# Layer 2's closing moved into its relu attention, with two chunks of the shared expert in the attention's end

## The chip, the cores and the metric

One NeuronCore of a Trainium2 chip runs the whole kernel as one launch. Its engines are TensorE (PE in the profile; its weight loads are PEld), VectorE (DVE), ScalarE (ACT), GpSimd (POOL) and the sync engine (SP), which here issues most DMA transfers. The metric is the device time of one execution in microseconds (us); lower is better. TensorE's clock has two levels, 1.2 and 2.4 GHz; the profile gives the granted clock as a share of the upper one, so that 0.50 is the lower level.

## The reference

A language-model tower of two layers on 4096 tokens (4 sequences of 1024) of width D = 192, all in float32. The change touches layer 2 alone:

```python
h = h + _L1_attn_ref(_layernorm(h), ...)   # relu ("performer") attention, 12 heads, 64 features:
    qp = relu(q @ projection.T) + 0.001;  kp = relu(k @ projection.T) + 0.001
    context = sum over tokens of kp x v;  out = (qp @ context) / (qp @ sum of kp)
    return out @ w_proj.T + b_proj                 # the output projection
h = h + _L1_ffn_ref(_layernorm(h), ...)    # mixture of experts:
    scores = softmax(xf @ w_router.T)              # router logits, top 2 of 8 experts
    out = routed + swiglu(xf; sg, su, sd)          # the shared expert: every token goes through it
```

## The kernel before

Tokens stand 128 to a tile, four tiles (CT) to a chunk of 512 (CHUNK), eight chunks (CHUNKS). The residual stream `h` stays in SBUF. Stages follow one another with a barrier of all engines between them. Each stage first takes its semaphores; SP sets each to its start value before the barrier. Inside a stage each engine has its own instruction list, written out in the source in a fixed order, and waits on semaphores; every engine works strictly in that order.

Layer 2 has four stages.

- `relu_attention`: a loop over chunks c, written out. In turn c TensorE makes the key features of c (`k_features`), turns a finished context (`turn_context`, only in even turns), projects queries and keys of c+1 (`project_qk`), forms the outputs of chunk c-2 (`outputs`), the query features of c in two halves of four and two pairs of heads (`q_features`), the values of c+1 (`project_v`), transposes the normed input of c+2, and adds chunk c to the context (`accumulate`). VectorE takes the key features out of PSUM with the relu, reads the context, norms chunk c+2 (`prepare`), divides chunk c-2 (`divide`, twice two tiles) and takes the query features out. ScalarE copies the projections and takes the square roots of the norm. Six PSUM banks form a ring: every unit of work (`qk`, `kf`, `qf`, `out`, `v`, `ct`) takes the next bank in one written order and waits until the unit that held it has been read. Banks 6 and 7 serve the transposes and the context.
- `close_attention`: projects the attention's rows with `w1_out`, adds them to `h`, norms the sum into `x2`, writes it to DRAM for the routed experts' gather, turns it (`transpose_x2`, into the shared expert's input `sh.xt`) and computes the router's logits. It works through eight chunks; layer 1 has the same stage. SP also loads the expert weights here.
- `route`: softmax, top 2, and the tables of which token goes into which block, almost all on VectorE. Beside it TensorE, ScalarE and GpSimd run chunks 0 and 1 of the shared expert. VectorE builds the rows of a table into `TABLE_BUFS` = 16 buffers, and TensorE multiplies them in between the shared units.
- `experts`: first shared chunk 2 (`ahead`), then a loop over pairs of blocks for the routed experts, then the tail: shared chunks 3 to 7 (`behind`), and for all eight chunks the mixing (`mix`) of the routed rows into `h`, which SP loads from DRAM into two buffers (`BUFS`), and the stores of the result.

A shared chunk is three units (24 in all). A unit is `shared_up` (four matmuls over 512 tokens), a silu on ScalarE, a product, and `shared_down`. In the tail VectorE's order is set by this rule, and SP loads chunk c+2's rows only after mixing chunk c:

```python
for n in behind:
    shared_product(nc, dve, s, n)
    if f == 0 and chunk > SHARED_AHEAD:
        shared_add(nc, dve, s, chunk - 1)
        until = min(CHUNKS, 2 * (chunk - SHARED_AHEAD))
        for c in range(chunks_mixed, until): mix(c)
for c in range(chunks_mixed, CHUNKS): mix(c)
```

Of the kernel before, what the change touches and what calls it, by code (L numbers as in the profile page):

```python
# [24 lines left out]
P = 128  # L25
# [25 lines left out]
SHARED_IN_ROUTE = 2  # L51
SHARED_AHEAD = 3
# [61 lines left out]
def pipeline(eng, turns, start, step, finish, unrolled=False):  # L114
# [8 lines left out]
    if unrolled:  # L123
        for i in range(turns - 1):
            turn(i)
    else:
        with eng.Fori(0, turns - 1) as i:
            turn(i)
    step((1, turns - 1), (0, turns - 1), None)
    finish()  # L130
# [552 lines left out]
def close_attention(nc, a, s, layer):  # L683

    with ExitStack() as ctx:
        new_sem = ctx.enter_context(semaphores(nc))

        def sb(name, shape, dt=F32):
            return ctx.enter_context(nc.sbuf_tensor(f"ca{layer}_" + name, shape, dt))

        h, attn, ps = s.h, s.attn, s.psum
        router = a[f"w{layer}_router"]
# [9 lines left out]
        if layer == 0:  # L702
            x2_t = sb("x2_t", [P, 2, 2, CHUNK])
        XB = P if layer == 0 else DB
        RB_AT = 0 if layer == 0 else DB
# [5 lines left out]
        weights, ones, chain = (new_sem(f"ca{layer}_{n}") for n in ("weights", "ones", "chain"))  # L711
        two = {n: [new_sem(f"ca{layer}_{n}{u}") for u in range(2)] for n in
# [10 lines left out]
        def x2_cols(u, k, w, rows_of=slice(0, P), j=0, n=CHUNK):  # L723

            if layer == 0:
                return x2_t[rows_of, u, w, j:j + n]
            first = k * S + (u * CHUNK + j)
            return s.shared.xt[rows_of, w, slice(first, first + n) if isinstance(k, int) else bass.ds(first, n)]

        @block.sync  # L730
        def _(sp):
            for dst, src in ((wo_a[:], a[f"w{layer}_out"][0:P, :]), (wo_b[:], a[f"w{layer}_out"][P:D + 1, :]),
                             (wr_a[:], router[0:P, :]), (wr_b[RB_AT:RB_AT + RB], router[P:, :])):
                sp.dma_start(dst, src).then_inc(weights, 16)
# [4 lines left out]
            tokens = s.x_tokens[layer].rearrange("(t p) d -> p t d", p=P)  # L739
# [24 lines left out]
        def _(dve):  # L764
            nc.vector.memset(rows_tb[DB:DB + 1, :, :], 1.0).then_inc(ones, 1)
            if layer == 0:
                nc.vector.memset(x2_t[DB:DB + 1, :, 1, :], 1.0).then_inc(ones, 1)

            def copy_x2(u, k):
                dve.wait_ge(two["x2_ps"][u], START + k + 1)  # L770
                dve.wait_ge(two["logits_ps"][u], START + k)
                rows_of = slice(0, DB if layer == 0 else P)
                nc.vector.tensor_copy(x2_cols(u, k, 1, rows_of), ps[rows_of, PS_XB, :]).then_inc(two["x2_dve"][u], 1)
# [36 lines left out]
        def _(act):  # L810
# [6 lines left out]
            def copy_x2(u, k):  # L817
                act.wait_ge(two["x2_ps"][u], START + k + 1)
                act.wait_ge(two["logits_ps"][u], START + k)
                nc.scalar.copy(x2_cols(u, k, 0), ps[:, PS_XA, :]).then_inc(two["x2_act"][u], 1)  # L820
# [10 lines left out]
            def start():  # L831

                act.wait_ge(ones, START + 2 - layer)
                copy_rows(0, 0)
# [3 lines left out]
        def _(pe):  # L838
            pe.wait_ge(weights, START + 64)
            pe.wait_ge(ones, START + 2 - layer)  # L840

            def transposes(src, bank_a, bank_b, first_b=P):
                for j in range(CT):
                    nc.tensor.transpose(ps[:, bank_a, j * P:(j + 1) * P], src[:, j, 0:P], s.ident[:])
                    last = nc.tensor.transpose(ps[0:D - first_b, bank_b, j * P:(j + 1) * P], src[:, j, first_b:D],
                                               s.ident[:])
# [8 lines left out]
            def transpose_x2(u, k):  # L855
# [3 lines left out]
                transposes(x2[:, u], PS_XA, PS_XB, XB).then_inc(two["x2_ps"][u], 1)  # L859
# [13 lines left out]
            def compute_logits(u, k):  # L873
# [3 lines left out]
                for j in range(CT):  # L877
                    dst = ps[:, PS_L, j * E:(j + 1) * E]
                    rows_of = slice(RB_AT, RB_AT + RB)
                    nc.tensor.matmul(dst, x2_cols(u, k, 0, slice(0, P), j * P, P), wr_a[:], start=True, stop=False)  # L880
                    last = nc.tensor.matmul(dst, x2_cols(u, k, 1, rows_of, j * P, P), wr_b[rows_of],
# [15 lines left out]
            pipeline(pe, B, lambda: transpose_rows(0, 0), step, finish, unrolled=(layer == 1))  # L897


class SharedExpert:  # L900
# [3 lines left out]
    PS_GATE, PS_UP, PS_Y = 1, 3, 5  # L904

    def __init__(self, sb, new_sem):
        self.xt = sb("xt", [P, 2, T])
        self.silu = sb("silu", [P, 2, CHUNK])
        self.up = sb("up", [P, 2, CHUNK])
        self.g = sb("g", [P, 2, CHUNK])  # L910
        self.y = sb("y", [P, CT * D])
        (self.gate_ps, self.up_ps, self.silu_done, self.up_left, self.g_done, self.down_done, self.y_copied,
         self.y_added) = (new_sem("sh_" + n) for n in (
             "gate_ps", "up_ps", "silu", "up_left", "g", "down", "y_copied", "y_added"))

    def units(self, first, last):

        return range(first * self.PARTS, last * self.PARTS)


def shared_up(nc, pe, s, n):
# [3 lines left out]
    gate, up = ps[:, sh.PS_GATE + n % 2, :], ps[:, sh.PS_UP + n % 2, :]  # L925
# [3 lines left out]
    pe.wait_ge(sh.g_done, START + n - 1 if n else START)  # L929
    nc.tensor.matmul(gate, s.up_a[:, 0, E, cols], x[0], start=True, stop=False)  # L930
    nc.tensor.matmul(up, s.up_a[:, 1, E, cols], x[1], start=True, stop=False)  # L931
    nc.tensor.matmul(gate, s.up_b[HIGH, E, cols], x[1][HIGH], start=False, stop=True).then_inc(sh.gate_ps, 1)  # L932
    nc.tensor.matmul(up, s.up_b[LOW, E, cols], x[0][LOW], start=False, stop=True).then_inc(sh.up_ps, 1)


def shared_down(nc, pe, s, n):

    sh, ps = s.shared, s.psum
    chunk, f = divmod(n, sh.PARTS)
    if f == 0:  # L940
# [1239 lines left out]
```

## Time and profile before

| | us |
|---|---|
| median of three runs | 1840.75 |
| the three runs | 1835.26 to 1847.22 |
| the profiled execution, its own time | 1849.49 |
| its span, first to last instruction | 1847.8 |
| busy in the span: TensorE / VectorE / ScalarE / GpSimd | 1621.7 / 1098.9 / 613.7 / 429.0 |

The busy times are shares of the whole span; the stages have different limits, so what a change in one stage is worth is read from that stage. Idle time of an engine that nothing waits for costs nothing.

### The profile page before, as it was taken

Reading aid. Unit: us, or ns where it says so; the run is one execution under the profiler, and the core shown is the slowest. Engines: PE = TensorE matmul, PEld = TensorE weight load, DVE = VectorE, ACT = ScalarE, POOL = GpSimd, SP = SyncE. Lnnn points to the kernel's source line nnn. Section 1 sums busy time; section 2 is a strip of 40 time slices with the busy share of each in tenths; the row PEclk is TensorE's granted clock in tenths of the full one; section 3 lists DMA queues with packets and bytes.
Section 4 is the critical chain, followed back from the end, with each engine's and each line's share of the span. In section 5 each row is a group of like instructions: output and inputs, shape, how many; then the busy total and the mean of one; then the engine's idle time right before and its main releaser. Section 6 shows DMA issues by size and latency. Waiting matters only on the chain. (4 is left out here: it accounts for less than half of the span.)

```text
span 1847.8 us, 28783 instructions
## 1 busy us (share of the span) xinstructions
PE 1621.7 (88%) x8964; PEld 889.3 (48%) x8965; DVE 1098.9 (59%) x2504; ACT 613.7 (33%) x826; POOL 429.0 (23%) x526
## 2 busy tenths in 40 slices
PE   5759999999899999675999918899699799999998
PEld 3411332233233232473666604667696656666654
DVE  5868998899799891365333335565355823333345
ACT  3411666566566668211111102111012112222111
POOL 6540000000000000101555414000001246666620
PEclk9765999899999999875999958999766799999999
DMA  2480222022222200720111121000420011111124
GB/s 81 148 142 12 35 35 33 4 35 34 35 34 35 35 1 1 212 64 7 39 40 41 36 60 43 2 1 2 120 100 26 1 30 53 52 51 52 46 81 147
DMA packets 64239, 92.82 MB, mean 50 GB/s; under 512 B 9809, under 2 KB 49556, under 8 KB 63124
## 3 DMA queue, kind: packets, MB, share of 16 engines
q1 hardware_dynamic: 50912, 65.08, 15.6%
q0 software_dynamic: 12288, 25.18, 4.6%
q10 hardware_dynamic: 960, 1.57, 0.5%
q8 instruction: 41, 0.67, 0.2%
q14 instruction: 38, 0.31, 0.1%
HBM read 61.82 MB, written 29.98 MB: 50 GB/s over the span
## 5 line engine op out<-in xcount | busy, mean ns | idle before, releaser
L510 DVE TENSOR_REDUCE sa_half_max<-psum 128x1 f32<-128x512 f32 x768 | 494.7, 688 | 79.9 <-PE psum L613 60.0
L567 ACT ACTIVATE sa_probs<-psum 128x1024 f32<-128x1024 f32 x384 | 372.5, 1021 | 168.1 <-PE psum L604 166.6
L613 PE MATMUL psum<-k_stack,q_stack 96*128 96x512 bf16 x768 | 286.4, 411 | 28.8 <-PEq L404 18.8
L604 PE MATMUL psum<-q_stack,k_stack 97*128 97x512 bf16 x768 | 232.1, 386 | 6.1 <-ACT sa_probs L567 5.4
L613 PEld LDWEIGHTS psum<-k_stack,q_stack 96*128 96x128 bf16 x768 | 75.2, 98 | 285.0 <-issue 153.1
L636 PE MATMUL psum<-sa_probs,sa_v_ext 128*32 128x512 f32 x1536 | 207.4, 612 | 0.6 <-ACT sa_probs L567 0.6
L1541 PE MATMUL psum<-w_e_up_a,ex_xt 128*128 x448 | 171.4, 525 | 0.0
L1405 ACT ACTIVATE ex_silu<-psum 128x384 f32<-128x384 f32 (+1 forms) x112 | 59.3, 529 | 289.4 <-PE psum L1541 286.9
L1557 PE MATMUL psum<-w_e_down,ex_g_t 128*128 x752 | 137.2, 334 | 0.5 <-DVE ex_g_t L1437 0.5
L1557 PEld LDWEIGHTS psum<-w_e_down,ex_g_t 128*128 128x128 f32 x752 | 120.7, 190 | 34.5 <-issue 34.5
L1445 DVE COPY ex_to_rows<-slot_rows 128x2 uint32 (+1 forms) x56 | 10.3, 184 | 211.6 <-DMA y_rows<-ex_y,ex_to_rows 117.5
L1347 POOL DMA_INDIRECT y_rows<-ex_y,ex_to_rows x112 | 110.3, 985 | 97.2 <-DVE ex_y L1446 69.1
L1316 POOL DMA_INDIRECT ex_x<-x_tokens,ex_tokens x112 | 110.7, 988 | 55.7 <-POOL ex_tokens L1322 40.1
L1430 DVE TENSOR_TENSOR ex_g<-ex_silu,psum 128x384 f32<-128x384 f32 (+1 forms) x112 | 67.1, 602 | 94.9 <-PE psum L1541 85.1
L499 POOL COPY sa_v_ext<-v_nat 128x512 f32 x12 | 7.2, 612 | 479.1 <-PE psum L636 478.7
L604 PEld LDWEIGHTS psum<-q_stack,k_stack 97*128 97x128 bf16 x768 | 72.8, 99 | 88.7 <-ACT sa_probs L567 28.9
L1541 PEld LDWEIGHTS psum<-w_e_up_a,ex_xt 128*128 128x128 f32 x448 | 83.7, 191 | 59.6 <-issue 31.0
L755 POOL COPY ca_rows<-attn 128x768 f32 (+1 forms) x16 | 13.2, 827 | 407.1 <-POOLq L715 311.8
L1534 PE MATMUL psum<-ex_w_b,ex_xt 64*128 64x384 f32 (+1 forms) x448 | 98.2, 557 | 3.1 <-ACT ex_xt L1399 2.3
L1399 ACT COPY ex_xt<-psum 128x512 f32<-128x512 f32 x56 | 32.8, 586 | 127.2 <-PE psum L1523 127.2
L1437 DVE COPY ex_g_t<-psum 128x384 f32<-128x384 f32 (+1 forms) x112 | 63.9, 605 | 17.3 <-PE psum L1548 14.7
L636 PEld LDWEIGHTS psum<-sa_probs,sa_v_ext 128*32 128x32 f32 x1536 | 30.4, 108 | 81.6 <-issue 75.5
(267 smaller groups left out, 2257.0 us busy)
## 6 DMA issues: line engine op xcount, KB each, us to landing
q_stack<-qk_parts SPq DMA_DIRECT2D x66, 128.0 KB, 4.5
k_stack<-qk_parts SPq DMA_DIRECT2D x66, 128.0 KB, 7.2
qk_parts<-ep_parts SPq DMA_DIRECT2D x16, 384.0 KB, 3.4
x_tokens<-x SPq DMA_DIRECT2D x16, 384.0 KB, 2.6
ex_rows<-y_rows SPq DMA_DIRECT2D x16, 384.0 KB, 4.7
qk_parts<-ep_parts SPq DMA_DIRECT2D x16, 192.0 KB, 4.3
w_e_down<-e_down SPq DMA_DIRECT2D x1, 3072.0 KB, 32.7
ra_rows<-y_rows SPq DMA_DIRECT2D x8, 384.0 KB, 3.3
```

Of the source, the lines that this page charges most:

```text
L510: nc.vector.tensor_reduce(half_max[:, g, hd, qt, half:half + 1], slot, AX.X, ALU.max).then_inc(ring_free[r], 1)
L567: nc.scalar.activation(probs[:, st % 2, 2 * pair:2 * pair + 2, :], ps[:, 2 * pair:2 * pair + 2, :], ACT.Exp, scale=SCALE0).then_inc(exp_do ...
L604: last = nc.tensor.matmul(ps[:, hd, :], kst[:, g, hd, kt * P:(kt + 1) * P], qst[:, g, hd, half * HALF:(half + 1) * HALF], start=True, stop ...
L613: last = nc.tensor.matmul(ps[:, 4 + r, :], qst[0:SK, g, hd, qt * P:(qt + 1) * P], kst[0:SK, g, hd, half * 512:(half + 1) * 512], start=Tru ...
L636: last = nc.tensor.matmul(ps[hd * W:(hd + 1) * W, OUT, :], v_ext[:, g, kt, hd, :], probs[:, st % 2, hd, :], start=(kt == 0), stop=(kt == T ...
L1316: pool.indirect_dma_start(out=x[:, u, :], out_offset=None, in_=x_tokens, in_offset=bass.IndirectOffsetOnAxis(ap=tokens[:, u:u + 1], axis=0 ...
L1347: pool.indirect_dma_start(out=y_rows, out_offset=bass.IndirectOffsetOnAxis(ap=to_rows[:, u:u + 1], axis=0), in_=y[:, u, :], in_offset=None ...
L1430: nc.vector.tensor_tensor(g[:, u, :], silu[:, u, :], ps[:, PS_UP + u, 0:F], ALU.mult).then_inc(g_done, 1)
L1437: nc.vector.tensor_copy(g_t[:, u, :], ps[:, PS_G + u, 0:F]).then_inc(g_t_done, 1)
L1534: last = nc.tensor.matmul(ps[:, bank + u, 0:F], xt[rows_of, u, v, :], w_b[rows_of, u, :], start=True, stop=False)
L1541: nc.tensor.matmul(ps[:, bank + u, 0:F], xt[:, u, v, :], w.up(u, v), start=False, stop=True).then_inc(done, 1)
L1557: last = nc.tensor.matmul(ps[:, PS_Y, u * D:(u + 1) * D], g_t[:, u, c * P:(c + 1) * P], w.down(u, c), start=(c == 0), stop=(c == FC - 1))
```

## The change

The stage `close_attention` of layer 2 is gone. Its steps become units of the attention's ring of six banks (`rows`, `po`, `x2`, `lg`) and stand in the lists of the attention's loop: in turn c the rows of chunk c-2 are transposed and projected, and chunk c-3 is normed (`statistics2`, `normalise2`), turned and given its logits. GpSimd's copy of the rows goes; VectorE writes the divided rows so that TensorE reads them directly. The copies of `x2` and of the logits, which VectorE had, go to ScalarE.

After the loop, chunks 5 to 7 are closed in a written-out end that also runs shared chunks 0 and 1 (units 0 to 5), each unit in one set of banks: gate and up in 6 and 7, the result in 4 and 5. There the ring has four banks (`FEWER`). The shared weights are a load of their own in the attention; the experts' weights are loaded in `route`, which no longer waits for them. `route` now has shared chunks 2 and 3 and 12 table buffers, `ahead` has chunk 4, the tail 5 to 7. `experts` itself is not edited. The core of the diff:

```diff
-SHARED_IN_ROUTE = 2
-SHARED_AHEAD = 3
+SHARED_IN_CLOSE = 2
+SHARED_IN_ROUTE = 4
+SHARED_AHEAD = 5
...
-        TABLE_BUFS = 16 if layer == 1 else 4
+        TABLE_BUFS = 12 if layer == 1 else 4
...
+                for dst, src in s.expert_weights:
+                    sp.dma_start(dst, src).then_inc(s.experts_loaded, 16)
...
     # TensorE's list, loop turn c
                 q_features(c)
+                if c >= 3:
+                    transpose_x2(c - 3)
...
                 if c + 2 < CHUNKS:
                     transpose(c + 2, 0)
+                if c >= 2:
+                    transpose_rows(c - 2)
                 accumulate(c)
                 if c + 2 < CHUNKS:
                     transpose(c + 2, 1)
+                if c >= 2:
+                    project_out(c - 2)
+                if c >= 3:
+                    compute_logits(c - 3)
     # its end (C5, C6, C7 are chunks 5, 6, 7)
+            shared_up(nc, pe, s, 0)
             turn_context(B - 1)
-            outputs(CHUNKS - 2)
-            outputs(CHUNKS - 1)
+            transpose_x2(C5)
+            outputs(C6)
...
+            shared_down(nc, pe, s, 0)
+            shared_up(nc, pe, s, 1)
+            outputs(C7)
+            transpose_rows(C6)
+            compute_logits(C5)
+            shared_down(nc, pe, s, 1)
+            shared_up(nc, pe, s, 2)
+            project_out(C6)
+            transpose_rows(C7)
+            shared_down(nc, pe, s, 2)
+            shared_up(nc, pe, s, 3)
+            project_out(C7)
+            transpose_x2(C6)
+            shared_down(nc, pe, s, 3)
+            shared_up(nc, pe, s, 4)
+            compute_logits(C6)
+            transpose_x2(C7)
+            shared_down(nc, pe, s, 4)
+            shared_up(nc, pe, s, 5)
+            compute_logits(C7)
+            shared_down(nc, pe, s, 5)
     # VectorE's list, loop turn c
+                if c >= 3:
+                    add_out(c - 3)
                 for p in range(PAIRS):
                     features(("kf", c, p), k_feat[:, c % 2, p, :])
                 if c and c % 2 == 0:
                     read_context(c // 2 - 1)
                 if c + 2 < CHUNKS:
-                    prepare(c + 2)
+                    statistics(c + 2)
+                if c >= 3:
+                    statistics2(c - 3)
+                if c + 2 < CHUNKS:
+                    normalise(c + 2)
+                if c >= 3:
+                    normalise2(c - 3)
                 if c >= 2:
                     divide(c - 2)
     # its end
+            add_out(C5)
+            statistics2(C5)
             read_context(B - 1)
-            divide(CHUNKS - 2)
-            divide(CHUNKS - 1)
+            normalise2(C5)
+            shared_product(nc, dve, s, 0)
+            divide(C6)
+            shared_product(nc, dve, s, 1)
+            divide(C7)
+            add_out(C6)
+            statistics2(C6)
+            shared_product(nc, dve, s, 2)
+            normalise2(C6)
+            shared_add(nc, dve, s, 0)
+            add_out(C7)
+            statistics2(C7)
+            shared_product(nc, dve, s, 3)
+            normalise2(C7)
+            shared_product(nc, dve, s, 4)
+            shared_product(nc, dve, s, 5)
+            shared_add(nc, dve, s, 1)
     # ScalarE's end
+            shared_silu(nc, act, s, 0)
+            root2(C5)
+            copy_x2(C5)
+            shared_silu(nc, act, s, 1)
...
```

## Rows read from the trace of the kernel before

**Rows 1.** Busy time by stretch: stretch, length, PE, PEld, DVE, ACT, POOL, clock, DMA.

```profile
1122.00:1294.50 172.50, 155.52 (x1790) 107.82 (x1789) 100.97 (x276) 28.95 (x57) 11.22 (x8) 0.96 0.02 6
1314.00:1412.20 98.20, 88.78 (x384) 83.71 (x384) 46.50 (x177) 14.68 (x32) 6.61 (x8) 0.60 0.40 115
1412.20:1474.30 62.10, 52.83 (x228) 36.38 (x228) 56.97 (x199) 11.14 (x19) 14.03 (x14) 0.80 0.00 1
```

**Rows 2.** Timeline of TensorE in the loop's turn c = 3: start, duration, what.

```profile
1199.23 5.50 PE L2007 MATMUL psum<-ra_context,ra_q_feat 128*128 128x102 f32 x48
...
1205.81 1.13 PE L1940 MATMUL psum<-ra_qk,ra_feat_b 32*128 32x512 f32 x4
```

**Rows 3.** Timeline of VectorE in turns 3, 4 and 7.

```profile
1196.04 1.13 DVE L92 BATCH_NORM_STATS2 ra_stats<-h 128x6 f32<-128x192 f32 x4
...
1200.24 0.18 DVE L103 RECIPROCAL ra_tmp<-ra_std 128x4 f32<-128x4 f32 x1 [2.39 <-ACT ra_std L1829]
...
1202.43 0.30 DVE L1802 RECIPROCAL ra_inv<-psum 128x24 f32<-128x24 f32 x1
...
1228.02 0.31 DVE L1802 RECIPROCAL ra_inv<-psum 128x24 f32<-128x24 f32 x1 [1.28 <-PE psum L2007]
...
1289.53 0.31 DVE L1802 RECIPROCAL ra_inv<-psum 128x24 f32<-128x24 f32 x1 [1.78 <-PE psum L2007]
```

**Rows 4.** Timeline of TensorE in layer 1's closing, one chunk.

```profile
804.18 0.27 PE L844 MATMUL psum<-ident,x 128*128 128x128 f32 x1
...
806.12 0.36 PE L880 MATMUL psum<-ca_wr_a,ca_x_t 128*128 128x8 f32 x2
...
807.90 0.57 PE L869 MATMUL psum<-ca_wo_a,ca_rows_ta 128*128 128x192 f32 x2
...
810.60 0.27 PE L844 MATMUL psum<-ident,x 128*128 128x128 f32 x1
```

**Rows 5.** Clock by stretch, and TensorE's timeline after three idle times.

```profile
795.00:815.00 20.00, 19.96 (x152) 19.31 (x152) 16.67 (x68) 5.56 (x12) 0.83 (x1) 1.00 0.19 59
1160.00:1165.00 5.00, 5.00 (x42) 3.70 (x44) 0.48 (x1) 1.45 (x3) 0.00 (x0) 0.50 0.01 3
...
1158.24 0.56 PE L1916 MATMUL psum<-ra_wv_full,ra_xt 128*128 128x192 f32 x2 [2.48 <-DVE ra_q_feat L1767]
...
1295.06 0.55 PE L1990 MATMUL psum<-ident,ra_ctx_t 128*128 128x128 f32 x3 [0.60 <-ACT ra_ctx_t L1870]
1298.24 12.59 PE L2007 MATMUL psum<-ra_context,ra_q_feat 128*128 128x102 f32 x96 [2.64 <-DVE ra_context L1788]
```

**Rows 6.** Timeline of TensorE in the tail, one shared unit.

```profile
1784.40 1.02 PE L930 MATMUL psum<-sh_xt,w_e_up_a 128*128 128x512 f32 x2
...
1787.27 1.57 PE L944 MATMUL psum<-w_e_down,sh_g 128*128 128x192 f32 x8
1788.67 1.02 PE L930 MATMUL psum<-sh_xt,w_e_up_a 128*128 128x512 f32 x2
```

**Rows 7.** The tail: VectorE's timeline, SP's, and the page's DMA issues (KB, us to landing).

```profile
1807.14 5.60 DVE L1464 SCALAR_TENSOR_TENSOR h<-ex_rows,gate,h 128x192 f32<-128x192 f32 x16
...
1813.88 0.69 DVE L964 TENSOR_TENSOR sh_g<-sh_silu,psum 128x512 f32<-128x512 f32 x1 [0.54 <-ACT sh_silu L955]
...
1842.70 1.02 DVE L974 TENSOR_TENSOR h<-h,psum 128x384 f32<-128x384 f32 x2 [2.00 <-PE psum L944]
...
1797.37 1.31 SPq L1374 DMA_DIRECT2D ex_rows<-y_rows  x2
...
ex_rows<-y_rows SPq DMA_DIRECT2D x16, 384.0 KB, 4.7
```

**Rows 8.** VectorE's first instruction of layer 2's route, by the timeline.

```profile
1413.86 0.42 DVE L1158 TENSOR_REDUCE ro_top<-logits 128x32 f32<-128x256 f32 x1 [1.72 <-PEq L1046]
```

**Rows 9.** ScalarE's timeline where its function changes.

```profile
1415.55 1.28 ACT L955 ACT_TABLE_LOAD   x1
```

**Rows 10.** Groups by line: busy us, mean ns, idle before.

```profile
L1240 DVE TENSOR_SCALAR ro_in_block<-ro_block_f,ro_place_block,ro_row_f 128x72 f32<-128x72 f32 (+1 forms) x96 | 30.5, 318 | 0.0
```

More of the change, by code:

```diff
@@ L122, in pipeline @@
     step((0, 0), None, (1, 0))
[L123 to L128, printed above, removed]
+    with eng.Fori(0, turns - 1) as i:
+        turn(i)
     step((1, turns - 1), (0, turns - 1), None)
@@ L710, in close_attention @@
         tmp = sb("tmp", [P, 2, CT])
-        weights, ones, chain = (new_sem(f"ca{layer}_{n}") for n in ("weights", "ones", "chain"))
-        two = {n: [new_sem(f"ca{layer}_{n}{u}") for u in range(2)] for n in
+        weights, ones, chain = (new_sem("ca_" + n) for n in ("weights", "ones", "chain"))
+        two = {n: [new_sem(f"ca_{n}{u}") for u in range(2)] for n in
                ("rows", "rows_ps", "rows_act", "out_ps", "var", "std", "x2", "x2_ps", "x2_act", "x2_dve",
@@ L924, in shared_up @@
     chunk, f = divmod(n, sh.PARTS)
-    gate, up = ps[:, sh.PS_GATE + n % 2, :], ps[:, sh.PS_UP + n % 2, :]
+    gate, up = (ps[:, bank, :] for bank in sh.banks(n)[:2])
     x = [sh.xt[:, w, chunk * CHUNK:(chunk + 1) * CHUNK] for w in range(2)]
@@ L939, in shared_down @@
     chunk, f = divmod(n, sh.PARTS)
+    y = sh.banks(n)[2]
     if f == 0:
@@ L970, in shared_add @@
     sh, ps = s.shared, s.psum
+    y = sh.banks(chunk * sh.PARTS)[2]
     dve.wait_ge(sh.down_done, START + sh.PARTS * (chunk + 1))
@@ L2009, in outputs, with transpose_tiles @@
                     last.then_inc(ring_full[bank(unit)], 1)
+            def transpose_tiles(src, units, cols):
+                claim(units)
+                for j in range(CT):
+                    for unit, part in zip(units, cols):
+                        ins = nc.tensor.transpose(ps[0:part.stop - part.start, bank(unit), j * P:(j + 1) * P],
+                                                  src[:, j, part], s.ident[:])
+                        if j == CT - 1:
+                            ins.then_inc(ring_full[bank(unit)], 1)
@@ new lines, in transpose_rows, with transpose_x2, project_out @@
+            def transpose_rows(c):
+                for i in range(2):
+                    pe.wait_ge(*left(("out", c, i)))
+                transpose_tiles(attn[:, c % 2 * CT:(c % 2 + 1) * CT, :], close_units(c, ["rows"]),
+                                (slice(0, P), slice(P, D)))
+            def transpose_x2(c):
+                pe.wait_ge(x2_done, START + c + 1)
+                transpose_tiles(x2[:, c % 2], close_units(c, ["x2"]), (slice(0, P), slice(DB, D)))
+            def project_out(c):
+                if c == 0:
+                    pe.wait_ge(out_weights, START + 64)
+                    pe.wait_ge(ones_row, START + 1)
+                for i in range(2):
+                    pe.wait_ge(*left(("rows", c, i)))
+                for i in range(2):
+                    unit = ("po", c, i)
+                    claim([unit])
+                    for j in range(2):
+                        toks = slice((2 * i + j) * P, (2 * i + j + 1) * P)
+                        dst = ps[:, bank(unit), j * D:(j + 1) * D]
+                        nc.tensor.matmul(dst, rows_ta[:, c % 2, toks], wo_a[:], start=True, stop=False)
+                        last = nc.tensor.matmul(dst, rows_tb[:, c % 2, toks], wo_b[:], start=False, stop=True)
+                    last.then_inc(ring_full[bank(unit)], 1)
```

337 lines of the change are left out of this document (235 added, 102 removed).

## The prediction

> **What bounds the kernel now.** I read the page's slices first, then busy time by stretch, then the timelines of the attention, the closing and the tail. The attention's loop is bound by TensorE: 155.5 of 172.5 us busy at a clock of 0.96, against 101.0 on VectorE [rows 1]. The closing behind it is also TensorE's, busy 88.8 of 98.2 us, but at a mean clock of 0.60 [rows 1]. Layer 1 does the same closing at 1.00 in 6.42 us a chunk (804.18 to 810.60) [rows 4, 5], so eight chunks are 51.4 us of work at full clock. That is what moving it can save. The closing ends at 1413.86 - 1.72 = 1412.14, with the logits' copy [rows 8]. The tail, too, is TensorE's: units follow every 4.27 us [rows 6], fifteen of them, and the mixing on VectorE fits between.
>
> **The loop.** Of one chunk's 6.42 us the two sets of transposes take 1.94, the logits 1.78, the projection 2.70 [rows 4]. Turn 2 gets rows and projection (0.97 + 2.70 = 3.7), turns 3 to 6 a whole chunk each (25.7), turn 7 up to its projection 4.6: 34.0 us, all on TensorE, which has no idle time to hide it.
>
> VectorE's new steps come before `divide`, whose banks the second half of the query features waits for. In turn 3 statistics take 1.8 us (1196.04 to 1200.24 - 2.39) and fit in the idle 2.39 [rows 3]. The second norm takes 2.19 (1200.24 to 1202.43) [rows 3] and delays the first divide by that. The second divide waited for the outputs anyway, 1.28 us in turn 4 [rows 3]; so TensorE, which had no wait there (1199.23 + 5.50 + a half of the features = 1205.81) [rows 2], now waits 0.9 in turns 3 and 5. Turn 4 has no such 2.39: 1.8 + 2.2 - 1.3 = 2.7. Turn 6 norms no new chunk, and the old one's 4.0 take that place: nothing. Turn 7 has 1.78 idle: 4.0 - 1.8 = 2.2 [rows 3]. Together 6.7. `add_out` (1.0) at a turn's head is covered by the logits on TensorE. The new ring claims wait for ScalarE copies of 0.6 us that end long before. SP's new loads stand behind the last row load, and its `x2` stores behind nothing that TensorE needs.
>
> The last `accumulate` ended at 1295.06 - 0.60 = 1294.46 [rows 5]. After the change the projection of chunk 5 ends at 1294.46 + 34.0 + 6.7 = 1335.2.
>
> **The end of the attention.** TensorE's list from there: four logits 7.1, six units of 4.27 are 25.6, two outputs of 5.50 are 11.0 [rows 2], two projections 5.4, five sets of transposes 4.9, the turned context 0.6: 54.5 us. Three waits stand in it, since products, norms and adds alternate on one VectorE:
> - `transpose_x2(C5)` waits for reading the context (2.64, TensorE's idle before the outputs [rows 5]) and the norm (2.19): 5.0 with its handovers. `outputs(C6)` and all behind it are queued there.
> - `shared_down` of unit 2 waits for the half add (0.6), statistics (1.8) and product (0.69 [rows 7]) after the projection of chunk 6, less the transposes between (0.97): 2.2. Unit 3 likewise behind chunk 7: 2.2.
>
> With the last add (1.02 [rows 7]) 64.9 us, to 1400.1. Single banks for gate and up cost nothing more, as TensorE has other steps between a unit's up and down.
>
> **Costs that the trace doesn't show.** Before the attention SP sets 17 more semaphores. The change of stage with 10 took 1.72 [rows 8], so between 0 and 17 x 0.17 = 2.9; I take 1.0, since those 1.72 are a barrier besides. ScalarE changes seven times between square root and silu, each a table load of 1.28 [rows 9]: 0 to 9.0. Each falls where I find ScalarE waiting for TensorE; I take 0.5.
>
> **The clock.** After an idle 2.48 us TensorE ran five of the next seven at 0.50 [rows 5], a loss of 2.5; after an idle 2.64 the 96 matmuls took 12.59 and not 11.0 [rows 2, 5], a loss of 1.6. The new order has one idle time of 5.0 and four of 2.2 to 2.7 (turns 4 and 7, units 2 and 3). Bounds 0 and 5 x 2.5 = 12.5; I take 2.5 and four times 1.5, 8.5 in all, since the cases in the trace lie in this size but not every idle need hit.
>
> A rule of the Trainium skill speaks against the change here ("TensorE: Matmul & The Clock Gate", "Part 4: PE-mode transpose"): transposes on TensorE don't count as activity for the clock. In layer 1's closing 1.9 us of transposes and 1.8 of logits per 6.42 held 1.00 [rows 4, 5], so there the rule doesn't decide; the lower clock of layer 2's closing fits it. By the rule the fourth rival below would come.
>
> So the attention with the closing ends at 1400.1 + 1.0 + 0.5 + 8.5 = 1410.1, where the closing ended at 1412.14: only **2.0 us** won. The full clock gives back some 37 us (88.8 busy against 51.4), and the barrier and weight load between the stages go; two shared chunks (25.6) and the waits use it up.
>
> **The route** keeps its six shared units and VectorE's chain, which bounds it (57.0 of 62.1 us busy [rows 1]). Twelve buffers for sixteen: VectorE may stand until TensorE is back from a unit, at most four rows of two builds, 8 x 0.318 = 2.5 [rows 10]. I take 1.0, as one unit of 4.27 is shorter than twelve rows. The expert weights now load here, seven of the eight megabytes that loaded within the closing; there the DMA engines were busy 0.40 of 98.2 us, 39 us in all, and in the route 0.00 of 62.1 [rows 1]: it is hidden by VectorE's chain. If it were not, TensorE would wait at the head of `experts`.
>
> **The tail.** Two chunks less are 6 x 4.27 = 25.6 us less on TensorE. But the rule of the mixing is unedited: with three chunks `mix` runs for chunks 0 and 1, then 2 and 3, and chunks 4 to 7 come after the last product. In the trace's times the second such stretch ends at 1807.14 + 5.60 = 1812.7, the last product at 1814.6 [rows 7]. Then a mix of 2.8 follows a load. A load goes out after the mix two chunks earlier; a store's and its own issue (0.65 each of 1.31) and landing (4.7) make 6.0 [rows 7]. Chunk 4: 1809.9 + 6.0 = 1815.9, mixed 1818.7; chunk 5: 1821.5; chunk 6: 1818.7 + 6.0 = 1824.7, mixed 1827.5; chunk 7: 1830.3; last add 1831.3. Before it ended at 1843.7 [rows 7]. So the tail wins **12.4** and not 25.6: what is late next is the mixing with its two buffers. Bounds: with no wait for a load 16.9; with one landing more 7.7.
>
> **The sum.** -2.0 + 1.0 - 12.4 = -13.4 us. On the profiled execution 1849.49 becomes 1836.1; that execution lies 8.7 above the median of the runs, so the median of 1840.75 becomes **1827**.
>
> **The rivals.**
> - The mixing hides and the tail wins all 25.6: 13.2 more, 1814. For it: VectorE is idle for half the tail. Against: four mixes are behind the last product in the list. 0.07.
> - The clock holds through the new idle times: 8.5 less, 1819. For it: the loop with its small waits as a whole holds 0.96 [rows 1]. Against: both cases over 2.4 us fell. 0.20.
> - VectorE becomes the loop's bound. Its add, statistics and norm (1.0 + 1.8 + 2.2 = 5.0) stand whole in TensorE's path in five turns: 25 where I count 6.7, and the clock falls in each: 12.5 where I count 3. That is 27.8 more, 1855, **slower** than before. It decides from the point where VectorE's chain from key features to the second divide no longer finds the idle 2.39, 1.28 and 1.78 [rows 3]. Against it: these rows. 0.08.
> - Transposes and 8-column logits let the clock fall in every turn and at three more places of the end: 2.5 each in five turns (3 counted) and 7.5, so 17 more, 1844. For it: 0.60 in layer 2's closing. Against it: 1.00 in layer 1's. 0.13.
>
> **How the numbers follow.** My forecast has the remaining 0.52: 1827. Its own costs reach from 1815 (no fall of the clock, better tail) to 1846 (all table loads on the path, poorer tail), which also takes in the second and the fourth rival; the first and the third lie outside with 0.15. Range 1815 to 1846. About 1% is what a measurement of this kernel tells from no change: under 1822 lie most of the second rival, the first and an edge of mine, 0.30; over 1859 an edge of the third, 0.05; 0.65 between.
>
> **What would show it.** In the new profile: the loop's turns 3 to 5 some 7 to 9 us longer, at a clock near 1.00; one idle time near 5 us before layer 2's `transpose_x2` of chunk 5 and two over 2 before `shared_down`, each with a lower clock after it; the route's first reduce within a few us of 1412; and a tail in which TensorE is done some 15 us before the last mix. I am wrong if the loop waits on VectorE every turn, if the end of the attention lies far from 1410, or if the mixing is through when the last unit is.

## The result, and the profile after

The changed kernel takes 1846.67 us (median of 20 runs, 1843.31 to 1856.69), the kernel before 1839.85 (20 runs, 1834.70 to 1850.38). The ratio is 1.0039, with a 95% interval of 1.0024 to 1.0054: **slower by 0.4%**, where I forecast 1827. That is just above the range of 1815 to 1846, and a change inside the 1% either way to which I gave 0.65. The profiled execution of after took 1844.46 us with a span of 1842.8. It is 5.0 shorter than the profiled execution of before, although the medians say that the change costs 7. That contradiction is the first thing to explain.

Busy time by stretch, kernel after (columns as in [rows 1]; turns 4 to 7 of the loop, then the loop up to the projection of chunk 5, then the end of the attention):

```profile
1225.66:1258.43 32.77, 31.67 (x292) 23.45 (x292) 19.75 (x70) 6.40 (x14) 0.00 (x0) 0.90 0.04 14
1258.43:1288.70 30.27, 28.26 (x289) 21.78 (x288) 17.24 (x54) 6.87 (x15) 0.00 (x0) 0.99 0.05 14
1288.70:1321.49 32.79, 32.23 (x285) 23.73 (x284) 16.30 (x52) 5.23 (x11) 0.00 (x0) 0.85 0.04 13
1321.49:1342.49 21.00, 20.55 (x237) 18.02 (x237) 13.24 (x35) 3.01 (x7) 0.00 (x0) 0.84 0.07 20
...
1124.40:1342.50 218.10, 201.48 (x2039) 148.81 (x2039) 124.03 (x377) 42.53 (x89) 10.76 (x8) 0.92 0.06 19
1342.50:1416.70 74.20, 63.21 (x332) 47.65 (x331) 25.95 (x93) 19.27 (x30) 0.00 (x0) 0.89 0.05 17
```

The loop is still TensorE's, but the clock is 0.92 where it was 0.96 [rows 1]. It falls in turns 0 and 1, as in the kernel before, and then in turns 4, 6 and 7. TensorE's timeline says where it falls (logits of chunk 3 and the head of turn 7; the first unit; the waits of the end; the head of the route; the tail's third unit, at full clock):

```profile
1320.85 0.39 PE L2216 MATMUL psum<-ra_wr_a,sh_xt 128*128 128x8 f32 x2
1321.17 0.39 PE L2217 MATMUL psum<-ra_wr_b,sh_xt 64*128 64x8 f32 x2
1321.49 1.38 PE L2114 MATMUL psum<-ra_feat_a,ra_qk 32*128 32x128 f32 x32
1322.65 1.92 PE L2114 MATMUL psum<-ra_feat_b,ra_qk 32*128 32x128 f32 x16
...
1344.92 1.12 PE L939 MATMUL psum<-sh_xt,sh_up_a 128*128 128x512 f32 x2
1345.88 1.58 PE L940 MATMUL psum<-sh_xt,sh_up_a 128*128 128x512 f32 x2
...
1355.19 1.97 PE L2177 MATMUL psum<-ident,x 128*128 128x128 f32 x8 [5.16 <-DVE x L110]
1356.95 6.89 PE L2168 MATMUL psum<-ra_context,ra_q_feat 128*128 128x102 f32 x48
...
1388.73 1.57 PE L954 MATMUL psum<-sh_down,sh_work 128*128 128x192 f32 x8 [2.40 <-DVE sh_work L974]
...
1399.16 1.54 PE L954 MATMUL psum<-sh_down,sh_work 128*128 128x192 f32 x8 [2.40 <-DVE sh_work L974]
...
1418.98 2.05 PE L939 MATMUL psum<-sh_xt,sh_up_a 128*128 128x512 f32 x2 [3.32 <-PEq L1058]
...
1790.47 1.02 PE L939 MATMUL psum<-sh_xt,sh_up_a 128*128 128x512 f32 x2
```

Two things are to be seen. Each pair of logits matmuls starts 0.32 us behind the last, so a chunk's logits take 2.5 us; in layer 1 the step takes 1.78 [rows 4]. And right behind the logits the same features take 1.92 us for sixteen where they take 1.06 at full clock. In this profile a fall comes after six of the eight logits steps; in the profile of a later kernel with the same attention ("Earlier mixing, four buffers") it comes after three. The three waits of the end are where I put them, at the size I gave them: 5.16 for 5.0, twice 2.40 for 2.2.

VectorE's timeline, after (the route's first reduce, [rows 8]; the tail's last mixes, [rows 7]):

```profile
1418.98 0.42 DVE L1172 TENSOR_REDUCE ro_top<-logits 128x32 f32<-128x256 f32 x1 [2.27 <-PEq L1058]
...
1821.67 2.85 DVE L1478 SCALAR_TENSOR_TENSOR h<-ex_rows,gate,h 128x192 f32<-128x192 f32 x8 [1.03 <-DMA ex_rows<-y_rows]
...
1830.44 2.85 DVE L1478 SCALAR_TENSOR_TENSOR h<-ex_rows,gate,h 128x192 f32<-128x192 f32 x8 [2.59 <-DMA ex_rows<-y_rows]
1834.36 2.85 DVE L1478 SCALAR_TENSOR_TENSOR h<-ex_rows,gate,h 128x192 f32<-128x192 f32 x8 [1.07 <-DMA ex_rows<-y_rows]
1837.24 1.02 DVE L985 TENSOR_TENSOR h<-h,psum 128x384 f32<-128x384 f32 x2
```

The attention ends at 1418.98 - 2.27 = 1416.7, 4.6 later than the closing did in the trace of before, where I forecast 2.0 earlier. From the route's first reduce to the third unit of the tail it is 371.5 us against 370.5 [rows 6, 8]. From there to the end of the last add it is 47.8 against 59.3 [rows 6, 7]: 11.5 won. So trace against trace the stages after the attention did what I said, and the attention with the closing took 6.6 more.

### The profile page after: what moved, and what is told of

Read it like the earlier page. It is cut to its first block and busy times, and to the rows that moved or that the text cites. A ratio compares the mean times of both kernels' runs of the same rounds, so it can differ in the third digit from the quotient of the medians.

```text
span 1842.8 us, 28573 instructions
## 1 busy us (share of the span) xinstructions
PE 1604.2 (87%) x8964; PEld 868.2 (47%) x8965; DVE 1090.2 (59%) x2488; ACT 628.0 (34%) x849; POOL 423.5 (23%) x518
## 5 line engine op out<-in xcount | busy, mean ns | idle before, releaser
L1419 ACT ACTIVATE ex_silu<-psum 128x384 f32<-128x384 f32 (+1 forms) x112 | 59.3, 529 | 290.0 <-PE psum L1555 287.4
L1451 DVE COPY ex_g_t<-psum 128x384 f32<-128x384 f32 (+1 forms) x112 | 63.7, 605 | 15.8 <-PE psum L1562 13.3
```

The costliest lines, as they stand in the source:

```text
L1451: nc.vector.tensor_copy(g_t[:, u, :], ps[:, PS_G + u, 0:F]).then_inc(g_t_done, 1)
```

## The experiments

### The kernel before, profiled again (three runs of the same kernel)

No edit. The question was where the profiled execution of before had lost the 9 us that lay above its median.

> The kernel before, unchanged, to see whether its profiled execution (1849.49 us, 9 to 10 above the median of its runs) is typical of it. Theory A: layer 2's closing is what differs between executions, because TensorE's clock there is sometimes low (0.60 in the profile, 98 us for eight chunks) and sometimes held as in layer 1's closing (1.00, 6.42 us a chunk). Then this profile, if its time is near 1840, shows a closing of some 88 to 90 us at a mean clock of 0.65 to 0.75 and all other stages as before within 1 us. Theory B: the closing is always at about 0.60 and 98 us, and what lies above the median was lost elsewhere, in layer 1 (softmax attention, experts); then the closing is 97 to 99 us again whatever the whole time is.

> The kernel before, unchanged, a third profile. Theory A: what differs between its executions is the clock in layer 2's closing: from the closing's first transpose to its end 93.5 us at a mean of 0.61 in the execution of 1849.49 us, 80.1 at 0.76 in the one of 1837.47. Then the rest of the execution (its time less the closing) is again 1756 to 1758 us, within 1.5 either way, whatever the time. Theory B: other stages vary as much; then the rest lies more than 3 us off.

> The kernel before, unchanged, a fourth profile, for the same question: by theory A the time less the closing is again 1756 to 1758 us, within 1.5 either way; by theory B it lies more than 3 us off.

The executions took 1837.47, 1835.08 and 1839.91 us. Busy time by stretch from the closing's first transpose to its end, first in the profiled execution of before (1849.49), then in these three, in order:

```profile
1318.60:1412.10 93.50, 88.78 (x384) 83.71 (x384) 45.55 (x176) 14.68 (x32) 4.96 (x6) 0.61 0.41 118
```

```profile
1320.80:1400.90 80.10, 73.62 (x384) 68.48 (x384) 44.78 (x176) 14.81 (x32) 4.97 (x6) 0.76 0.47 139
```

```profile
1317.30:1398.80 81.50, 74.70 (x384) 69.48 (x384) 44.62 (x176) 14.82 (x32) 4.96 (x6) 0.75 0.46 136
```

```profile
1317.60:1403.80 86.20, 79.69 (x384) 74.17 (x384) 44.88 (x176) 14.71 (x32) 4.96 (x6) 0.70 0.44 128
```

The same 384 matmuls take 80 to 93.5 us, at a clock of 0.76 to 0.61. The time less the closing is 1756.0, 1757.4, 1753.6 and 1753.7: it varies by 3.8 us (more than the 1.5 of theory A, so other stages have a small share), the closing by 13.4. The first of the three is even shorter than I expected: 84.7 us on the measure of its expectation (80.1 and the 4.6 before the first transpose), not 88 to 90. The profile from which I predicted shows the longest closing of the four. With some 1755 beside it, the median of 1840 has a closing of about 85.

### Logits over full rows

```diff
+            nc.vector.memset(wr_b[LOW], 0.0).then_inc(ones_row, 1)
...
-                    last = nc.tensor.matmul(dst, sh.xt[HIGH, 1, toks], wr_b[HIGH], start=False, stop=True)
+                    last = nc.tensor.matmul(dst, sh.xt[:, 1, toks], wr_b[:], start=False, stop=True)
```

> The kernel after, with the second matmul of each logits step over all 128 rows (the weight's lower 64 rows are zeros) and not over the upper 64 rows. Theory A: the logits are what lowers TensorE's clock in the loop and the end, since the clock is low right behind six of the eight logits steps in the trace of the kernel after. With full rows a step takes 1.8 us as in layer 1 and not 2.5, 8 x 0.7 = 5.6 less, and the falls of the clock behind it go or get rarer, some 2 to 2.5 each of six: 12 to 15 less. Together 18 to 20 less than the kernel after, 1826 to 1829. Theory B: the waits (0.66 to 0.78 in turns 3 to 5, 5.16 and twice 2.40 in the end) are what lowers it; then only the 5.6 of the step's own length go, 1841, and the mean clock in turns 4, 6 and 7 stays at 0.84 to 0.89.

1839.22 us (12 runs), ratio to before 0.9987 (0.9964 to 1.0010). Against the 1.0039 of after that is 0.52% or 9.6 us less, between the two theories. TensorE's timeline, then the busy time of turns 4 to 6:

```profile
1225.71 0.37 PE L2218 MATMUL psum<-ra_wr_b,sh_xt 128*128 128x8 f32 x2
1225.93 0.37 PE L2217 MATMUL psum<-ra_wr_a,sh_xt 128*128 128x8 f32 x2
...
1243.84 1.13 PE L2102 MATMUL psum<-ra_qk,ra_feat_b 32*128 32x512 f32 x4 [2.24 <-DVE attn L1890]
...
1328.38 1.13 PE L2102 MATMUL psum<-ra_qk,ra_feat_b 32*128 32x512 f32 x4 [2.23 <-DVE attn L1890]
```

```profile
1226.46:1259.27 32.81, 29.23 (x292) 22.50 (x291) 19.66 (x70) 6.56 (x14) 0.00 (x0) 0.95 0.05 14
1259.27:1288.68 29.41, 27.41 (x289) 21.08 (x288) 17.24 (x54) 6.88 (x15) 0.00 (x0) 1.00 0.05 14
1288.68:1317.47 28.79, 27.06 (x284) 20.56 (x283) 16.31 (x52) 5.31 (x11) 0.00 (x0) 1.00 0.05 15
...
1245.50:1248.90 3.40, 3.40 (x15) 2.51 (x14) 1.77 (x3) 1.07 (x2) 0.00 (x0) 0.50 0.00 0
```

The pairs now follow every 0.22 us, and no fall of the clock stands right behind the logits in the loop. The waits show that I had forecast behind the divide: 2.24 in turn 4 (2.7 forecast), 2.23 in turn 7 (2.2). What turn 4 loses (0.95) is one short fall right behind its wait, the last row; behind the wait of turn 7 the clock holds here. The three later kernels with full-row logits in the attention (both of "Together" and the last experiment) show the same fall in turn 4 and one behind the wait of turn 7 too. In the first of "Together":

```profile
1327.13 1.53 PE L2087 MATMUL psum<-ra_qk,ra_feat_b 32*128 32x512 f32 x4 [2.23 <-DVE attn L1889]
1328.59 1.97 PE L2163 MATMUL psum<-ident,x 128*128 128x128 f32 x8
```

The features take 1.53 for 1.13 there, and the transposes 1.97 for 1.04. From the head of turn 2 (1170.30) to the end of the projection of chunk 5 (1337.24) it takes 166.9 us; the same stretch up to the last accumulate took 126.5 in the trace of before. That is 40.4 more, the fall in turn 4 included, and my terms were 34.0 + 6.7 = 40.7. In the kernel after it was 47.2.

### Logits twice over

The same kernel with the eight full-row matmul pairs done twice on the same place.

```diff
-                for j in range(CT):
+                for n in range(2 * CT):
+                    j = n % CT
```

> The kernel after with full-row logits (as in e2) computed twice over, the second time onto the same place: 1.8 us more of 8-column matmuls in each of the eight steps, longer than the 2.5 of the kernel after, but none over 64 rows. Theory A: the form over 64 rows is what brings the clock down; then it holds here in turns 4 to 7 at 0.95 to 1.00, and the kernel takes 8 x 1.78 = 14.2 more than e2, 1853. Theory B: it is the time spent in 8-column matmuls, of whatever rows; then the clock falls behind the logits as in the kernel after (turns 4, 6 and 7 at 0.84 to 0.89) or more often, 6 to 12 more on top: 1859 to 1866.

1858.59 us (4 runs), ratio 1.0088 (1.0053 to 1.0123): 1.01% or 18.6 us more than with the logits once, for 14.2 of work. The time lies between the theories; the clock decides. Busy time of turns 4 to 7:

```profile
1226.96:1263.69 36.73, 35.64 (x308) 27.23 (x307) 19.75 (x70) 6.39 (x14) 0.00 (x0) 0.83 0.04 12
1263.69:1297.36 33.67, 32.47 (x305) 24.99 (x305) 17.24 (x54) 6.87 (x15) 0.00 (x0) 0.89 0.04 13
1297.36:1330.68 33.32, 32.78 (x300) 24.71 (x300) 16.30 (x52) 5.23 (x11) 0.00 (x0) 0.87 0.04 14
1330.68:1360.00 29.32, 28.86 (x275) 23.69 (x276) 15.49 (x45) 4.47 (x9) 0.00 (x0) 0.80 0.05 15
```

No matmul of the logits is over 64 rows here, and the clock is low in all four turns. So it falls without that form. This kernel differs from the last by the number of pairs alone, so it is the longer stretch of them that brings the falls. The other profiles with the same loop bear this out. Take the logits of chunks 0 to 3. None of 16 steps of 1.8 us (four kernels) has a fall in it or right behind it. Of 12 steps of 2.5 us (the kernel after, "No shared units" and "Earlier mixing") 8 have one, and so have all four of 3.6 us here. Not counted is one fall in turn 6 of three kernels with 1.8 us: it comes 4.3 us behind the logits, right behind an idle time of 1.3. The transposes are the same in all of them. Whether 64 rows add to it at equal length isn't shown.

### The same edit in the kernel before

Layer 2's closing there has the same logits over 64 rows. The edit is that of the full rows above, in `close_attention`:

```diff
+            else:
+                nc.vector.memset(wr_b[0:DB], 0.0).then_inc(ones, 1)
...
-                    rows_of = slice(RB_AT, RB_AT + RB)
+                    rows_of = slice(0, RB if layer == 0 else P)
```

> The kernel before with the second matmul of layer 2's logits over all 128 rows (lower 64 rows of the weight zero), nothing else. Theory A: the matmuls over 64 rows are what lets TensorE's clock fall in layer 2's closing, and fall for a different time in each execution. Then the closing runs like layer 1's, 6.4 us a chunk, most of it at a clock near 1.00: from its first transpose to its end some 62 to 66 us, where the two profiles of the kernel before show 93.5 and 80; the median is 15 to 20 less than the kernel before, 1822 to 1827, and the runs lie closer together. Theory B: the form only makes the step longer (2.5 us and not 1.8 a chunk) and the clock goes its own way: 5.6 less, 1836, with the same spread of some 18 us between the runs.

1831.88 us (12 runs, 1826.79 to 1839.61), ratio 0.9948 (0.9927 to 0.9970). Busy time of the closing in its profile:

```profile
1317.60:1392.40 74.80, 65.51 (x384) 61.59 (x384) 44.37 (x176) 14.80 (x32) 4.96 (x6) 0.77 0.50 148
...
1317.60:1335.30 17.70, 15.35 (x53) 14.04 (x54) 6.24 (x22) 2.33 (x5) 1.66 (x2) 0.50 0.99 256
1335.30:1383.10 47.80, 43.94 (x307) 41.89 (x305) 34.93 (x143) 11.69 (x25) 3.31 (x4) 0.93 0.39 128
```

Theory A goes too far: the clock is 0.77, as in the better executions of before, and not near 1.00. The rows say where. The closing begins at 0.50, behind an idle time of 7.8 us that ends with the load of the router's weights, and stays there for 17.7 us; it ends with 9.3 us at 0.50; between them it runs at 0.93. In the four profiles of before it begins at 0.50 too, for 10.5 to 18.9 us. So the length of the logits isn't all that lowers the clock there: the closing starts low, as a stage of its own behind that idle time. The closing is 5.3 shorter than the 80.1 at 0.76, which is the step's own length (5.6). The median falls by 9.6, more than that; whether the clock is higher on average in the other executions isn't shown by one profile.

### No shared units in the end of the attention

```diff
-SHARED_IN_CLOSE = 2
-SHARED_IN_ROUTE = 4
-SHARED_AHEAD = 5
+SHARED_IN_CLOSE = 0
+SHARED_IN_ROUTE = 2
+SHARED_AHEAD = 3
...
-            shared_up(nc, pe, s, 0)
             turn_context(B - 1)
             transpose_x2(C5)
             outputs(C6)
-            shared_down(nc, pe, s, 0)
-            shared_up(nc, pe, s, 1)
             outputs(C7)
...
-            slot = n % SLOTS if n < len(order) else (n - len(order)) % FEWER
+            slot = n % SLOTS
...
```

The units' products, adds and silus go from the lists of VectorE and ScalarE as well.

> The kernel after without the six shared units in the end of the attention: chunks 0 and 1 of the shared expert in the route, 2 ahead, 3 to 7 in the tail, as before; the closing stays in the attention, and its end keeps the six banks. Theory A: the six units cost their length less the waits that they cover. In the end there is then 2.4 + 0.6 + 1 + 11 + 1 + 2.5 + 2.7 + 1 + 2.7 + 1 + 2.5 + 1 + 2.5 = 32 us of work on TensorE and waits for VectorE of some 9.7 (context and norm of chunk 5), 3 (norm of 6) and 5 (norm of 7), with 4 to 8 for the clock: the attention ends about 56 us behind the loop's last projection instead of 74, 18 earlier. The tail is 11.6 longer again. In all 6 less than the kernel after, 1840. Theory B: the end is bound by VectorE's chain whatever TensorE does, so the units are free there; then the end is only 4 to 6 us earlier and the whole 6 more than the kernel after, 1853.

1833.40 us (12 runs), ratio 0.9954 (0.9931 to 0.9977): 0.85% or 15.7 us less than after, and **faster than before** by 0.5%. TensorE's timeline from the logits of chunk 4 to the head of the route, and the busy time of that stretch:

```profile
1340.81 0.28 PE L2201 MATMUL psum<-ra_wr_a,sh_xt 128*128 128x8 f32 x2
...
1349.59 1.97 PE L2162 MATMUL psum<-ident,x 128*128 128x128 f32 x8 [5.16 <-DVE x L110]
1373.91 0.98 PE L2189 MATMUL psum<-ra_wo_a,ra_rows_ta 128*128 128x192 f32 x2 [1.04 <-ACT ra_rows_ta L1961]
...
1394.46 2.05 PE L939 MATMUL psum<-sh_xt,sh_up_a 128*128 128x512 f32 x2 [2.47 <-PEq L1058]
...
1340.81:1394.46 53.65, 42.89 (x237) 40.45 (x236) 20.01 (x83) 6.53 (x18) 0.02 (x1) 0.68 0.07 23
```

From logits to route it is 53.7 us; with the six units it was 1418.98 - 1342.49 = 76.5. The units cost 22.8 of their 25.6 there. They hide no wait: TensorE is idle for 10.8 us of this stretch without them, and for 13.3 with them. What they give back is clock, which is 0.68 without them and 0.88 with them. The wait of 5.16 is the same with them and without, as `shared_up(0)` stands ahead of the turned context, which the wait is for, and `shared_down(0)` behind it. The waits for the norms of chunks 6 and 7 that I expected to come out here (3 and 5) are 1.0 to 1.1 and for ScalarE's copies. Theory A had the direction, but its 6 was too small: the waits that I gave 17.7 us come to 8.3, and the lower clock takes back about half of the difference (51.2 us to the end of the attention, where I had 56). The profiled execution is 12.1 us shorter than that of after, the runs say 15.7; with intervals of some 4 us that is no contradiction.

### Earlier mixing, four buffers

`MIXED_BY` says how many chunks are mixed once each of the tail's nine products is through.

```diff
-            BUFS = 2
-            rows = sb("rows", [P, BUFS, k_top, CT, D])
+            BUFS = 4
+            MIXED_BY = (0, 0, 0, 2, 2, 4, 4, 6, 6)
+            rows = s.attn[:].rearrange("p (b k j) d -> p b k j d", b=BUFS, k=k_top)
...
-                    until = min(CHUNKS, 2 * (chunk - SHARED_AHEAD))
+                until = MIXED_BY[n - behind[0]]
...
```

> The kernel after with four buffers for the routed rows in the tail (in the memory of the attention's rows, which nobody uses any more) and the mixing put behind products 4, 6 and 8 of the nine, two chunks each, the last two chunks behind the last product. Theory A (my step on the tail): what ends the tail is the mixing with its two buffers. Then the waits for loads (1.0, 0.5, 2.6, 1.1 in the trace of the kernel after) go and VectorE mixes beside TensorE's units; the last add comes at about 1829 in the times of that trace and not at 1837.2: 8 to 9 less, 1838. Theory B: the loads or the stores of the result bound the tail, or VectorE's mixing makes TensorE wait for the products; then at most 3 less, 1844 to 1847.

1836.43 us (12 runs), ratio 0.9981 (0.9958 to 1.0004): 0.58% or 10.7 us less than after. Tail, TensorE's first unit, then VectorE's end:

```profile
1778.82 1.02 PE L939 MATMUL psum<-sh_xt,sh_up_a 128*128 128x512 f32 x2
```

```profile
1818.00 5.60 DVE L1479 SCALAR_TENSOR_TENSOR h<-attn,gate,h 128x192 f32<-128x192 f32 x16
1823.64 1.02 DVE L985 TENSOR_TENSOR h<-h,psum 128x384 f32<-128x384 f32 x2
```

The last two mixes start without waiting for a load, and the tail is 45.8 us from its first unit to the last add's end. In the kernel after it was 55.0. That is 9.2 for the 8 to 9 of theory A: the mixing, by its rule and with its two buffers, was the bound. Which share the buffers have and which the earlier place in the list isn't shown, as the edit changes both.

The attention has the instructions of the kernel after, and yet its end is another in this profile (from the logits of chunk 4 to the head of the route):

```profile
1341.64:1413.50 71.86, 58.60 (x332) 44.92 (x332) 25.98 (x93) 19.29 (x31) 0.00 (x1) 0.98 0.06 17
```

It takes 71.9 us at 0.98 here and 76.5 at 0.88 in the profile of after. So what the clock costs in this end differs by some 5 us from one execution to the next.

### Together

The full-row logits without shared units in the end; and, as the other way, the kernel after with full-row logits and earlier mixing. The edits are those above.

> The closing inside the attention without shared units in its end (as e3), with full-row logits (as e2). Theory A: both gains add up, since they lie in different places: e3 lies 0.85% under the kernel after and e2 0.52%, together 1.37% of 1846, 25 less: 1821 to 1826, 0.6 to 1.1% under the kernel before. Theory B: with the units gone the end of the attention waits for VectorE (5.2 before the turning of chunk 5), and a shorter logits step there only makes a wait longer; then only the loop's part counts, 4 x 0.7 and two falls of the clock: 1828 to 1830.

> The kernel after with full-row logits (as e2) and four buffers and earlier mixing in the tail (as e4). Theory A: the two gains lie in different stages and add up: 0.52% and 0.58% of 1846, 20 less: 1825 to 1829, some 0.7% under the kernel before, and within 5 us of e7, which has two shared chunks more in its tail (66.5 against 45.8 us, as e3 and e4 show) but 24.5 us less in the attention's end. Theory B: what a stage wins is lost elsewhere and the kernel stays at or above 1835.

1824.55 us (6 runs), ratio 0.9906 (0.9877 to 0.9936), and 1826.53 (7 runs), ratio 0.9933 (0.9903 to 0.9964). Against after that is 1.33% (24.6 us, 25 expected) and 1.06% (19.6, 20 expected): the gains add up. The two ways to split the shared chunks lie 2 us apart by the medians and 5 by the ratios, which the intervals don't separate. The traces say what is behind it: from the logits of chunk 4 to the head of the route it is 45.8 us without the units (1337.18 to 1383.02) and 71.3 with them (1337.88 to 1409.17), so the six units cost 25.5 of their 25.6, and the tail with the earlier mixing wins 66.5 - 45.8 = 20.7.

The first of the two also repeats the moved closing at another length of the logits. Against the kernel before with the same full-row logits (0.9948) it is 0.42% faster, as it was 0.46% with the logits over 64 rows; here the intervals overlap slightly.

### The outputs ahead of the turning

```diff
-            transpose_x2(C5)
             outputs(C6)
+            transpose_x2(C5)
...
```

> The kernel of e7 with outputs(C6) ahead of transpose_x2(C5) in TensorE's list and in the ring: it needs the read context alone and not the norm of chunk 5 too. Theory A (my step on the wait of 5.0): the idle time of 5.5 before transpose_x2(C5) is reading the context and then the norm, one behind the other, and the outputs queued behind it pay for the norm; now TensorE waits some 2.7 us before the outputs and the norm runs beside them: 2.5 to 3 less, and up to 2.5 more if the clock no longer falls behind the wait: 1820 to 1822. Theory B: VectorE's chain bounds the end, so that the wait only moves to a later step (the divide of chunk 6 comes behind the norm on VectorE): within 1 us of e7.

1821.60 us (6 runs), ratio 0.9908 (0.9885 to 0.9931), the same as the 0.9906 without the edit. TensorE's timeline without it, then with it:

```profile
1344.88 1.97 PE L2163 MATMUL psum<-ident,x 128*128 128x128 f32 x8 [5.47 <-DVE x L110]
1346.65 11.61 PE L2154 MATMUL psum<-ra_context,ra_q_feat 128*128 128x102 f32 x96
```

```profile
1339.83 8.37 PE L2154 MATMUL psum<-ra_context,ra_q_feat 128*128 128x102 f32 x48 [2.96 <-DVE ra_context L1870]
1348.04 1.04 PE L2163 MATMUL psum<-ident,x 128*128 128x128 f32 x8
1348.91 5.50 PE L2154 MATMUL psum<-ra_context,ra_q_feat 128*128 128x102 f32 x48
```

The wait is 2.5 shorter, as theory A said, so it was context and norm one behind the other. But the first outputs now take the lower clock, 8.37 where 5.50 is full; without the edit the transposes took a part of it. Of 2.5 some 1.3 are left by the end of the attention, which the timing doesn't resolve.

## Why the prediction was wrong, step by step

**The step that failed** is the one from the profiled execution to the median: "that execution lies 8.7 above the median of the runs, so the median of 1840.75 becomes 1827". It takes for granted that what made the execution long stays in the kernel. The four profiles show that it lay in layer 2's closing (93.5 us at 0.61; 80 to 86 at 0.70 to 0.76 in the others), and that is the stage that the change removes. I counted its slowness twice: first as part of what the change saves, then as a surplus to take off the result. Without the second count my sum says 1836.1. My own rows held the warning: I noted 0.60 here and 1.00 in layer 1 [rows 1, 5] and asked only what the difference would give back, not whether every execution has it. The full clock was to give back "some 37 us"; in the median execution, with a closing near 85, it is 8 less. Of the 19.3 us between forecast and result 8.7 are this step, 6.6 the attention (the next two points), 0.9 the tail and 2.2 the distance of after's profiled execution below its own median; the last 0.9 lie outside these stages.

**The logits** were mis-sized: I took 1.78 us a chunk from layer 1 [rows 4], whose second matmul is over 65 rows:

```profile
806.34 0.37 PE L881 MATMUL psum<-ca_wr_b,ca_x_t 65*128 65x8 f32 x2
```

Layer 2's is over 64, and its step takes 2.5: eight times 0.7 is 5.8 of the 6.6 by which the attention ended later than I said. The 0.7 is the form's: with 128 rows the pairs follow every 0.22 us and not every 0.32. The Trainium skill ("TensorEngine Tiling (Array Packing)", "Key Properties") says that a change of tiling mode lets TensorE run empty first; alternating 128 and 64 rows is such a change, and the 0.10 us a pair agrees with it.

**The clock** cost more than my 8.5, and in other places. The attention took 16.7 us more than its work and waits (40.7 + 64.9); 5.8 are the logits, 0.8 the later start less turn 1's shorter time (below), which leaves some 10. But of the waits that I had in the loop, 6.7, only 2.1 came (0.66, 0.78 and 0.65 in turns 3 to 5), since a slower TensorE gives VectorE the time. So the clock itself took some 15 us in this execution, by subtraction. That some 10 are left, near my 8.5, is luck: lost clock and missing waits cancel in part.

I put the falls behind the new waits. From turn 2 on, all but one stand behind the logits; the wait of 5.16 did cost what I gave it: 1.97 and 6.89 for 1.04 and 5.50, 2.3 for 2.5. The mechanism that I named is there all the same: with the logits at 1.8 us the loop's waits of 2.2 come back, and a fall stands behind seven of the eight in four profiles. What I lacked was the falls behind a logits step of 2.5 us, which came first and took the place of those waits.

My fourth rival had transposes and logits as the cause; of the two it is the logits whose length decides. That its 1844 lies close to the result is luck: without the 8.7 taken off it would have said 1853. The rule behind it, that transposes don't count as activity (Trainium skill, "TensorE: Matmul & The Clock Gate", "Part 4: PE-mode transpose"), doesn't decide here, since the same transposes run in turns at 0.92 to 1.00 when the logits are short.

**What held**, term by term: the loop's work and waits (40.7 forecast, 40.4 with the short logits); the three waits of the end (5.0, 2.2, 2.2; measured 5.16, 2.40, 2.40); six units at full length (25.6; they cost 22.8 where they also raise the clock, 25.5 with the short logits, and so more than the tail gives back); the route (1.0 and 1.0); the tail (12.4; 11.5) with the mixing as what is late next, which four buffers and the earlier place confirm. The head of turn 0 came 2.4 later (1124.37 for 1121.98; 1.7 of it is the idle time before the first transpose, 41.05 for 39.31), where I had 1.0 for the semaphores; then turn 1 ran 1.6 shorter, as the fall of the clock behind its wait, 6.8 us long in the trace of before [rows 5], was 3.4 long here.

So the balance that I should have struck is this. Moving the closing into the loop wins: alone it takes 0.46% off the kernel before. Moving two shared chunks out of the tail into the attention's end loses 0.85%: 22.8 us there for 11.5 in the tail, by the traces, as the tail's new bound is the mixing. I had both numbers (25.6 and 12.4) and set the first against a closing that was 8 us too long.

**What stays open**: what decides in one execution of the kernel before whether the closing's clock is 0.61 or 0.76, how the shorter logits change that on average, and why the same logits steps have a fall behind them in one execution and not in another.

## What to carry to other kernels

When a profiled execution lies well off the median, find the stage that holds the difference before the sum is made; if the change touches that stage, the offset can't be carried over to the result. A duration is borrowed from another stage only where shapes agree down to the rows: 64 and 65 rows differed by 40% here. And work that is moved "into the waits" has to stand in the list between what starts the wait and what ends it; ahead of it, it adds its whole length, as `shared_up` of unit 0 did ahead of the wait of 5.16. And where a clock falls is read from more than one profile: the same end of the attention ran at 0.88 and at 0.98.

## What the runs showed of the hardware

TensorE's clock fell right behind stretches of 8-column matmuls in which it had no idle time, and more often the longer they were: in the loop behind none of 16 of 1.8 us, 8 of 12 of 2.5 and 4 of 4 of 3.6. It also fell behind single waits of 2.2 us, seven of eight where the stretches were short. And the closing, whose every chunk holds such a stretch of 2.5 us, takes 80 to 93.5 us for the same instructions, from one execution to the next. Padding 64 rows with zeros to 128 made a step shorter (1.8 for 2.5 us), with more arithmetic in it.
